# Two attention and expert layers on one core: the last sums made in the output tensor

## What is computed

```python
x = x + cross_attention_0(layernorm(x), ctx)   # 16 heads of 16, 375 keys for each sequence
x = x + ffn_0(layernorm(x))                    # 64 experts, 8 chosen for a row, inner width 128, and a shared expert
x = x + cross_attention_1(layernorm(x), ctx)
x = x + ffn_1(layernorm(x))                    # 8 experts, 2 chosen for a row, inner width 704

# ffn_1, for each row of xt:
w, idx = top_k(softmax(xt @ Wg.T), 2);  w = w / w.sum()
y = sum over the 2 chosen e of  w_e * (silu(xt @ W1[e].T) * (xt @ W3[e].T)) @ W2[e].T
```

## Time and profile before

| | |
|---|---|
| median of 3 runs | 1362.74 us (1360.32 to 1367.02) |
| span of the profiled execution | 1311.0 us |
| first experts | about 400 to 640 us of the span |
| second experts | about 1042 to 1302 us |
| last add issued | 1298.5 us |
| copy to `out` issued | 1302.3 us |
| copy landed | 1308.4 and 1310.6 us |
| end of the span | 1311.0 us |

### The profile page before, as it was taken

One profiled execution on the slowest core, in us unless ns is written; L12 is line 12 of the kernel. 1 busy time (PEld: TensorE's weight loads), 2 busy tenths in 40 slices (PEclk: granted clock), 3 DMA queues, 4 the chain that ended last, 5 costly groups with the idle time before them and its releaser, 6 DMA issues. The chain is left out here.

```text
span 1311.0 us, 40484 instructions
## 1 busy us (share of the span) xinstructions
PE 1221.2 (93%) x12894; PEld 949.1 (72%) x12895; DVE 829.9 (63%) x2657; ACT 495.5 (38%) x1255; POOL 539.5 (41%) x691
## 2 busy tenths in 40 slices
PE   5999999999977999999879999999999889999995
PEld 3666666666645988888556666666666889999995
DVE  3468777787767666666475777787865444444442
ACT  2454545454421434344224545554543121222121
POOL 1135656656473001100476676766522213333331
PEclk9999999999979999999979999999996999999998
DMA  4334444446545678865333333333324113354322
GB/s 113 104 118 145 133 148 137 144 134 203 152 136 184 200 203 235 262 187 160 105 87 91 99 104 101 93 101 97 87 56 181 54 38 101 100 161 115 101 35 81
DMA packets 115803, 166.65 MB, mean 127 GB/s; under 512 B 26480, under 2 KB 96768, under 8 KB 114672
## 3 DMA queue, kind: packets, MB, share of 16 engines
q0 software_dynamic: 22672, 58.41, 16.6%
q1 hardware_dynamic: 46496, 54.35, 14.3%
q10 hardware_dynamic: 46560, 52.98, 12.5%
HBM read 87.82 MB, written 63.49 MB: 115 GB/s over the span
## 5 line engine op out<-in xcount | busy, mean ns | idle before, releaser
L1047 DVE TENSOR_REDUCE mx<-banks 112x2 f32<-112x750 f32 x256 | 235.9, 936 | 93.1 <-PE banks L627 79.6
L1898 POOL DMA_INDIRECT xs_d<-xns,idx x160 | 155.6, 973 | 159.9 <-PE banks L653 113.9
L1567 ACT ACTIVATE shared_buf<-banks 125x672 f32<-125x672 f32 x256 | 173.1, 728 | 99.3 <-PE banks L653 98.2
L1912 POOL DMA_INDIRECT kept<-y_d,yidx x128 | 125.5, 980 | 115.4 <-issue 86.7
L919 PEld LDWEIGHTS banks<-xT,attn_buf 128*128 128x128 f32 x1364 | 158.7, 194 | 5.1 <-DVE xT L1433 3.6
L919 PE MATMUL banks<-xT,attn_buf 128*128 128x128 f32 x1364 | 159.0, 277 | 3.4 <-DVE xT L1433 3.4
L864 PE MATMUL banks<-xT,staged 128*128 128x128 f32 x1064 | 142.6, 277 | 7.1 <-DVE staged L1444 6.8
L864 PEld LDWEIGHTS banks<-xT,staged 128*128 128x128 f32 x1064 | 129.2, 192 | 11.9 <-DVE xT L1433 8.2
L653 PE MATMUL banks<-attn_buf 18*125 18x112 f32 x3072 | 121.5, 288 | 11.1 <-DVE mx L1047 6.4
L2064 POOL DMA_INDIRECT acc<-shared_buf,ids x31 | 57.9, 1866 | 166.9 <-ACT shared_buf L1798 127.4
L653 PEld LDWEIGHTS banks<-attn_buf 18*125 18x125 f32 x3072 | 98.7, 188 | 36.4 <-issue 18.0
(11 more groups left out here) (214 smaller groups left out, 1959.7 us busy)
## 6 DMA issues: line engine op xcount, KB each, us to landing
shared_buf<-xs_d SPq DMA_DIRECT2D x136, 128.0 KB, 2.4
y_d<-shared_buf ACTq DMA_DIRECT2D x132, 128.0 KB, 2.5
ringbuf<-in_we SPq DMA_DIRECT2D x6, 2176.0 KB, 8.2
ringbuf<-in_we POOLq DMA_DIRECT2D x32, 384.0 KB, 4.6
attn_buf<-attn_buf SPq DMA_DIRECT2D x128, 93.8 KB
attn_buf<-in_ctxT ACTq DMA_DIRECT2D x29, 375.0 KB
xs_d<-zrow ACTq DMA_DIRECT2D x16, 512.0 KB
y_d<-zrow ACTq DMA_DIRECT2D x16, 512.0 KB
```

What stands on the lines that cost most here:

```text
L1047: dve.tensor_reduce(mx[:, i % 2, 2 * p:2 * p + 2], banks[0:Q, 2 * p:2 * p + 2, 0:S], AX.X, ALU.max).then_inc(s_max, 1)
L1567: act.activation(pT[:, slot:slot + 2, :], banks[0:KT, first_bank:first_bank + 2, 0:ST * Q], ACT.Exp, scale=0.25).then_inc(s_exp, 1)
L1898: pool.indirect_dma_start(xs_d[L.number], bass.IndirectOffsetOnAxis(ap=idx[:, b % 2, k:k + 1], axis=0), rows, None).then_inc(s_scat[b % 2] ...
L1912: pool.indirect_dma_start(yg[:, u, k, :], None, y_d, bass.IndirectOffsetOnAxis(ap=yidx[:, u, k:k + 1], axis=0)).then_inc(s_gat[u][k * 4 // ...
```

## The change

The tensor `out` gets the 128 spare rows and takes the place of `acc`: residual, zeros and adds go to `out`, and the host takes its first 1792 rows. The semaphores `s_fin` and `s_out`, the two copies and SP's wait for them are gone. POOL's wait for the last add is still there, as its last instruction before the end of the block.

A second thing changes with it. The counts that are only used in waits (table rows 2 and 3) are no longer read by `table_values` but by a new helper, `counts`, which makes one load and one range check for each value.

```diff
@@ the output
-def build(nc, a, out):
+def build(nc, a, acc):
-        acc = nc.dram_tensor("acc", [TB + P, D], F32, kind="Internal").ap()
-    out = nc.dram_tensor("out", (B, Q, D), F32, kind="ExternalOutput").ap()
+    out = nc.dram_tensor("out", (TB + P, D), F32, kind="ExternalOutput").ap()
-    return r.results[0]["out"]
+    return r.results[0]["out"][0:TB].reshape(B, Q, D)
@@ the helper
+        def counts(handle, row, first, count, top):
+            return [handle.value_load(tabr[0:1, row, bass.ds(first + k, 1)], min_val=0, max_val=top) for k in range(count)]
@@ SP, first experts
-                    needs = table_values(SP, 2, first, EDGE, L.E)
+                    needs = counts(sp, 2, first, EDGE, L.E)
@@ SP, second experts
-                        done = table_values(SP, 3, i * L.ring + (TT // 2 + s), 1, L.tiles + 1)[0]
+                        done = counts(sp, 3, i * L.ring + (TT // 2 + s), 1, L.tiles + 1)[0]
@@ SP, end
-            sp.wait_ge(s_fin, 1)
-            sp.dma_start(result[0:P // 2], added[0:P // 2]).then_inc(s_out, 16)
-            sp.wait_ge(s_out, 32)
@@ DVE, second experts
-                    return list(zip(cols, table_values(DVE, 2, first, count, L.E)))
+                    return list(zip(cols, counts(dve, 2, first, count, L.E)))
@@ ACT, end
-            act.wait_ge(s_fin, 1)
-            act.dma_start(result[P // 2:], added[P // 2:]).then_inc(s_out, 16)
@@ POOL, end
                 pool.wait_ge(s_add, pool.snap((total >> 2) * 64 + 48))
-                pool.sem_inc(s_fin, 1)
```

More of the change, by code:

```diff
@@ L288, in build @@
         s_gat = [[sem(f"gathered{u}_part{p}") for p in range(4)] for u in range(2)]
-        s_w8, s_acc, s_add, s_fin = sem("weights_in_rows"), sem("residual_out"), sem("tile_added"), sem("all_added")
+        s_w8, s_acc, s_add = sem("weights_in_rows"), sem("residual_out"), sem("tile_added")
         s_cmb = sem("combined")
@@ L306, in build @@
         s_sgu, s_ssil, s_sh, s_sdn, s_sev = (sem(x) for x in ("sh_up_mm", "sh_silu", "sh_h", "sh_down_mm", "sh_ev"))
-        s_out = sem("out_done")
         s_held = [sem(f"held_{e}") for e in ("sync", "vector", "gpsimd")]
@@ L380, in weights_in @@
                     eng.dma_start(bo[l][:, :], a[f"{n}{l}"].partition_broadcast(Q)).then_inc(s, 16)
-        added = acc[0:TB, :].rearrange("(p r) d -> p (r d)", p=P)
-        result = out.rearrange("b q d -> (b q) d").rearrange("(p r) d -> p (r d)", p=P)
         block = ctx.enter_context(nc.Block())
```

## The result

Measured side by side, 13 executions each, the kernel took 1362.98 us before and 1372.97 us after (medians). The ratio is 1.0079, with a 95% interval from 1.0049 to 1.0108: **slower**, by 7 to 15 us. The prediction was 1357.0 us with a range of 1353.5 to 1362.

The account below looks back on a forecast made before the run. TensorE was taken as busy nearly throughout, followed by a 14 us tail of which the copy was 8.3. The terms 8.2 - 1.8 - 0 - 0.7 gave 5.7 us less than 1362.74, forecasting 1357.0 us, range 1353.5 to 1362.

Parts of the forecast that it names:

- The copy goes: Kernel's end: without the two copies the span ends just after the last add lands, 8.2 us less.
- the end is POOL's own: Rival, kernel's end: POOL's DRAIN takes 8.24 us even without the copy, 1365.2 us, no change; chance 0.06.
- The opening: Start of the second experts: four checked loads on DVE replace one load of four counts, uncovered, 1.8 us more, once.
- The seven turns: Second experts' turns: DVE 2.1 us later in each, covered by 2.6 us of slack before TensorE waits, costing nothing.
- SP in the first experts: First experts: SP's four checked loads make it 2.2 us later at each group's first tile load, 0.7 us more overall.
- the price of a value: One checked load of one value: 0.65 us on SP, 0.7 us on DVE, or 0.8 us there in a turn.
- My upper bound of 4.8: First experts: if landing times stayed as they are, six of 136 loads would be late by 4.8 us in sum.
- What lies around the span: Time outside the profiled span: 51.7 us, taken to stay unchanged.
- The sum: Whole kernel: 8.2 - 1.8 - 0 - 0.7 = 5.7 us less, 1357.0 us.
- the slower rival: Rival, second experts' turns: dearer DVE loads outrun the cover, 13 us lost there in all, 1372.7 us; chance 0.05.

Follow-up runs that it names:

- after: The changed kernel itself, against the kernel before: 1372.97 us, ratio 1.0079.
- masked_copy: Kernel before, copy kept, four counts still read in one load but each ANDed with 1023, plus one semaphore increment on SP: 1363.15 us, ratio 1.0014.
- after_third: The changed kernel run once more, on chip 4: 1321.54 us, ratio 1.0055 to the kernel before.
- masked_out_b: masked_out run once more, on chip 4: 1313.48 us, ratio 0.9998 to the kernel before.
- sp_checked: masked_copy with single checked loads for SP's four counts in the first experts alone, without the increment there, on chip 8: 1319.76 us, ratio 1.0032.
- dve_checked: masked_copy with single checked loads for DVE's counts alone, on chip 8: 1316.98 us, ratio 1.0005.
- group_checked: The changed kernel with its counts read four in one load and all four still checked: 1317.74 us, ratio 1.0024 to the kernel before.
- sp_twice: The changed kernel with SP reading and checking its four counts twice in the first experts: 1379.36 us, one execution.
- masked_out: The changed kernel, no copy, but counts read four in one load and ANDed with 1023 instead of checked: 1362.56 us, ratio 1.0000 to the kernel before.

## Why the prediction was wrong, step by step

- **The copy goes, -8.2 us: wrong, and the largest error.** The step that failed is "allowing 0.1 us more for POOL's own DRAIN". The DRAIN takes 8.24 us of its own and ends the kernel with or without a copy. The rival "the end is POOL's own" described exactly this and got 0.06. What misled me was one coincidence: 1302.4 + 8.2 and 1302.3 + 8.3 are the same moment. Two events that end together in one profile are no evidence of which waits. The rule that I weighed there, the Trainium skill, "Perfetto Trace Analysis", section "Per-engine timelines", that such a row shows execution and no wait for semaphores, agrees with the 11 traces of changed or altered kernels in which POOL had waited ahead of its DRAIN: 8243 ns in each. In the two where it had not, the row is 9.4 us long and its first 1.2 us run beside POOL's own last add, with 8.25 us behind it; so a row can hold time in which its engine's earlier work still runs.
- **The opening, +1.8 us: right**, 1.5 measured (idle 3.4 to 4.9). DVE's single load took 0.307 us instead of the 0.435 that I had taken from rows 9, and its checks 0.2 as assumed, so a value costs 0.63 us, not 0.7. The floor of 600 ns that the Trainium skill gives for a `tensor_load` ("DMA: Bandwidth & Descriptors", section "Latency and other measured facts") does not hold here: 0.27 us on SP, 0.31 on DVE.
- **The seven turns, 0: right.** DVE was to be 2.1 us later under a cover of 2.6; it was 1.8 us later (3.84 against 2.07), and TensorE's idle time in the turns grew by nothing beyond the opening's 1.5.
- **SP in the first experts, +0.7 us: the place, the sign and the price of a value right, the size wrong.** Measured are 4.9 us between `after` and `masked_copy`, 6.8 between `after_third` and `masked_out_b` on chip 4, 9.1 between `sp_checked` and `dve_checked` on chip 8 (1.7 of them by the clock). My upper bound of 4.8 was close to the least of them. The price of a value (0.65 us) was right. Wrong was "it catches up at the second and third, because it waits for TensorE between them". The view of SP's waits, which I had not read for this, has the answer: 90.5 us of waiting over 33 groups is 2.7 us in a group, and the change takes 2.2 of them. Half a microsecond is left in the average group. Three views bear this out: with the single checked loads 18.4 us of waiting are left in `after` and 22.6 in `sp_checked`; `group_checked`, which adds 1 us to a group, leaves 57.4 and loses nothing; `sp_twice` leaves 4.9 and loses 51. My reading of how the loss arises, that SP has nothing to catch up with where a tile comes late and carries its lateness into the next group, fits these but was not traced tile by tile. I compared each load's margin with one delay, as if every load began on time.
- **What lies around the span, 51.7 us: wrong**, 2.1 us. It did not enter the sum, but it should have warned me that the rows and the median were not of one kind of execution.
- **The sum.** With the DRAIN read rightly and SP at its measured size it is 0 + 1.5 + 0 + 4.9 = 6.4 us more, just under the 6.7 to 14.7 of the measured interval. I gave slower 0.05 because I let the copy's 8.2 us stand against every loss; without them nothing in the case could gain. That the slower rival named 1372.7 us and 1372.97 were measured is luck: it put 13 us into the seven turns, where nothing was lost, and took the 8.2 us off.

**What stays open.** On chip 4 the stages account for the loss: 6.8 + 1.5 = 8.3 us there, 8.1 between the medians of `after_third` and `masked_out_b`, and 4.5 to 9.9 by the ratio of `after_third`. Where the kernel before takes 1363 us (chip 0, and the comparison of the result) they give 6.4 us, or 8.0 with the slow stretch in the group of 44, while the medians say 10, 11 and 14. The rest may lie in the second attention, which took 441.1, 446.8 and 453.3 us in the three profiles with checked loads and 439.1 and 435.5 in the two without; the granted clock there was 0.91, 0.89 and 0.89 against 0.91 and 0.92. On chip 8 it took 406.9 us with SP's checked loads and 405.0 to 408.9 without. Single profiles of a stage that varies this much can't settle whether the later start of that attention costs it clock or whether this is scatter, and no run here was made to tell.

## What to carry to other kernels

Before costing the removal of the last transfer, ask what else would still end at that time: here an engine's DRAIN of 8.24 us ran beside it and was just as long, and the way to shorten the end was to take waits off that engine. For a producer that issues loads ahead, don't compare one delay with the margin of one load, but the added time of a whole round with all the waiting that the producer does in a round; when little of that is left, the next small addition costs tens of microseconds. And see that the profile and the times come from the same chip: a gap of 50 us between span and median is itself a finding.

## What the runs showed of the hardware

- POOL's DRAIN at the end of the block took 8243 ns in every kernel in which POOL first waited for its last DMA, with and without a copy in flight, and 9433 and 9438 ns in the two in which it began 1.2 us before POOL's last work was over. What it does in that time no run shows; in this kernel POOL issues the indirect DMAs, and no kernel without them ran. ACT's DRAIN took 8 ns without the copy and 0.63 to 0.64 us right behind the issue of its half of the copy.
- A table load from SBUF costs SP 0.27 us for one value and 0.29 for four; DVE 0.31 for one and 0.96 for four. A range check costs 0.15 and 0.02 us on SP, 0.19 and 0.02 on DVE.
- The same kernel took 1363 us on one chip and 1315 us on two others. `masked_out`, on chips 0 and 4, has first experts equal to 0.1 us, and attentions that are 15 and 32 us longer on chip 0, the second at a granted clock of 0.92 instead of 0.97.
